# The feed-forward's input scale and rounding, moved from the attention steps into the preparation

## The chip, the core and the metric

The kernel runs on one core of one Trainium2 chip. The metric is device time in microseconds (us) from the start to the end of one execution; before the change it is 664.96 us, the median of 3 runs (664.12 to 666.36).

## What is computed

One transformer layer on x of shape (2, 1024, 256). The layer-normalised x goes to two branches that do not depend on each other, and the output is x plus both.

```python
xn = layernorm(x)                     # over the last axis, 2048 tokens of 256
# attention: 16 query heads, 4 key/value heads, causal, low-rank projections, rotary part of 64
# feed-forward with dynamic int8 rounding:
def dyn_quant_linear(x, w, b):
    sx = max(max(abs(x)) / 127, 1e-8)             # ONE scale for the whole tensor
    qx = clip(round(x / sx), -127, 127)
    sw = max(max(abs(w), axis=1) / 127, 1e-8)     # one scale per output channel
    qw = clip(round(w / sw[:, None]), -127, 127)
    return (qx @ qw.T) * (sx * sw) + b
h   = gelu(dyn_quant_linear(xn, w1, b1))          # w1: 1024 x 256
out = x + attention(xn) + dyn_quant_linear(h, w2, b2)
```

The scale sx needs the largest absolute value of the whole of xn, so nothing of xn can be rounded before all of it is normalised.

## The kernel before, in words

Five engines run their own programs and meet at semaphores. The order of each program is written out by hand; nothing is scheduled by a planner. There are three parts.

*Preparation* (from 0 to 69.7 us). The array `acc` (128 partitions, 16 tiles of 256) holds x, in four parts of 4 tiles. VectorE normalises it in place (`statistics`, `layernorm`, line 785), TensorE transposes it (`turn_xn`, line 1144), ScalarE and VectorE split the transposed values into a high and a low half (`xt_hi`, `xt_lo`), TensorE multiplies them down (`down`), and again both halves are stored (`down_low`, lines 809 to 813). Beside it the weights of the four key groups are folded: `turn_weights(g)`, `join_weights(g)` into PSUM bank 6, ScalarE's `weight_high(g)` (lines 611 to 617) and VectorE's `weight_low(g)` (lines 822, 825). GpSimd rotates and splits the first query (`rotate`, `split_query`, lines 490 to 508).

*Attention*, 32 steps (one head of one batch each) and a tail step. A step has six slots (`UNITS`), with two or one query tiles each. In a slot TensorE does `scores` (lines 1116 through `mm`), then values of the step before; VectorE does `maxima` (line 918) and, one slot later, `low` (line 926); ScalarE does `exponentials` (lines 700, 706); SyncE transposes the result by DMA (lines 374, 380). Scores of a unit wait for the `low` of the unit three before it. GpSimd turns the query of the step after next: four products of 2.3 to 2.4 us, a cast and a subtraction (line 508, which sets `qlo_done`; a step's first scores wait for it).

Work that belongs to no unit goes through "misc" entries: TensorE fills PSUM bank 6 or 7, alternately, and another engine empties it. `misc_of(n)` lists the entries of step n with their slots, in order, from a usual part and the table `EXTRA`; an entry waits (`misc_free`) until the entry two before it, which had the same bank, is emptied. Kinds: `query` (emptied by ScalarE, line 635), `turn` (the attention output of a pair of heads; emptied by ScalarE into o_hi and by VectorE into o_lo, line 950), `out`, `ka`, `kb`, and for the feed-forward `w` (transposed rounded weights, line 1382), `xmax` (the maxima of all partitions turned into a row by TensorE, `spread_rows`, line 1239) and `x` (transposed rounded xn, line 1375, emptied by ScalarE into `qx_t`, line 646).

The feed-forward's input is made ready inside the attention steps on VectorE: `largest(t)` (line 836) reduces a part of acc to its largest absolute value per partition, in slots 1 to 4 of step 2 (`LARGEST_AT`); line 1054 reduces the four; entry `xmax` in slot 5 spreads them; `activation_scale` (lines 987 to 991) makes sx, s1 = w1s * sx and 1/sx; `round_part(t)` (line 1010) rounds a part of acc in place, in slots 0, 2, 4 and 5 of step 3 (`ROUND_AT`). After the last `x` entry, in step 4, SyncE reloads x into acc (line 399), and the first additions of attention output to it come in step 5, slot 3 (line 956).

The scales of w1 and w2 are made in step 1 (`weight_largest`, lines 972 to 974), and GpSimd rounds both (lines 525, 529).

*Feed-forward and tail* (after 603 us): products, Gelu, scale, second rounding, output.

Of the kernel before, what the change touches and what calls it, by code (L numbers as in the profile page):

```python
# [117 lines left out]
def build(nc, x, w_kv_down, w_k_nope, w_k_rope, w_v, w_q_down, w_q_nope, w_q_rope, w_o, w1, b1, w2, b2,  # L118
          cos_rows, sin_rows, out):
    with ExitStack() as ctx:  # L120
# [638 lines left out]
        def _(dve):  # L759
# [223 lines left out]

            def activation_scale(idx):

                dve.wait_ge(S["misc_full"], idx + 1)
                dve.tensor_reduce(sm["xall"], misc_bank(idx)[:, 0:P], AX.X, ALU.max).then_inc(misc_used(idx), 1)
                dve.wait_ge(misc_used(idx), USERS_AHEAD[idx] + 1)
                chained(dve.tensor_scalar(sm["sx"], sm["xall"], 1.0 / QMAX, Q_EPS, ALU.mult, ALU.max))
                dve.tensor_scalar(sm["s1"], sm["w1s"], sm["sx"], None, ALU.mult)  # L990
                chained(dve.reciprocal(sm["rsx"], sm["sx"]))
# [13 lines left out]

            def round_part(t):

                part = acc[:, PT * t:PT * (t + 1), :].rearrange("p t d -> p (t d)")
                dve.wait_ge(S["xt_psum"], 2 * NPART)
                dve.tensor_scalar(part, part, sm["rsx"], MAGIC, ALU.mult, ALU.add).then_inc(S["x_rounded"], 1)  # L1010
# [503 lines left out]
```

## Time and profile before

| | us |
|---|---|
| median of 3 runs | 664.96 (664.12 to 666.36) |
| the profiled execution | 664.83 |
| its span, first to last instruction | 662.7 |
| busy: TensorE / VectorE / ScalarE / GpSimd | 581.1 / 524.5 / 460.4 / 459.7 |

The profile is of one execution. Its span is the time from the first to the last instruction; 2.1 us of the execution lie around it. In it PE is TensorE (PEld its weight loads), DVE VectorE, ACT ScalarE, POOL GpSimd, SP SyncE; PEclk is the clock granted to TensorE, 1.00 for 2.4 GHz and 0.50 for 1.2 GHz. A step is counted here from the start of its first `maxima` on VectorE: step 2 is 110.27 to 132.66 us, step 3 to 152.00, step 4 to 170.44.

### The profile page before, as it was taken

How to read it: one execution, taken by the hardware profiler on the slowest of the kernel's cores; microseconds unless marked ns; L12 is line 12 of the kernel's file. 1: busy time of each engine (PE TensorE's matmuls, PEld its weight loads, DVE VectorE, ACT ScalarE, POOL GpSimd, SP SyncE). 2: the span in 40 equal slices, each digit the busy share in tenths (PEclk: the TensorE clock that was granted, in tenths of full speed). 3: DMA queues.
4: the chain of work that ended last, by engine and by line, in shares of the span. 5: the costliest groups of instructions: out<-in, count | busy, mean ns of one | idle time of the engine just before them, and what ended most of it. 6: DMA issues, size and time to landing. Idle time of an engine off the chain costs nothing.

```text
span 662.7 us, 15774 instructions
## 1 busy us (share of the span) xinstructions
PE 581.1 (88%) x6288; PEld 423.3 (64%) x6288; DVE 524.5 (79%) x824; ACT 460.4 (69%) x712; POOL 459.7 (69%) x258
## 2 busy tenths in 40 slices
PE   7888888687979979997998899889899988986967
PEld 5566455465757657765776677667667765765536
DVE  5933778996768978897888788887988888885885
ACT  3445657668856867786778877876877688765762
POOL 3267777957766688768878977877797789730326
PEclk9868987989999989997999999999999999996979
DMA  9772796778999798899999999999999989998003
GB/s 258 231 238 82 184 195 119 122 141 168 211 161 170 156 166 155 147 156 182 167 163 154 170 154 171 159 180 168 163 157 165 160 154 157 156 155 141 17 1 127
DMA packets 323607, 104.13 MB, mean 157 GB/s; under 512 B 305808, under 2 KB 316624, under 8 KB 323408
## 3 DMA queue, kind: packets, MB, share of 16 engines
q1 hardware_dynamic: 322752, 102.54, 82.9%
q8 instruction: 50, 0.82, 0.5%
q10 hardware_dynamic: 784, 0.59, 0.3%
q14 instruction: 21, 0.17, 0.1%
HBM read 19.21 MB, written 8.39 MB: 42 GB/s over the span
## 4 chain that ended last, share of the span: by engine, by line
PE 39%; DVE 30%; ACT 10%; issue 8%; DMA 7%; POOL 4%; SPq 1%; DVEq 0%; POOLq 0%; ACTq 0%
PE psum L1116 36%; DVE small L918 10%; DVE p_src L926 8%; DMA pt<-p_src 5%; ACT psum L706 5%; ACT p_src L700 3%; DMA acc<-in_L_attn_x 3%; DVE o_lo L950 2%; PE psum L1329 1%; DVE small L1063 1%; SPq L380 1%; DVE o_norm L943 1%; DVE acc L785 1%; DVE acc L956 1%; POOL q_raw L496 1%
## 5 line engine op out<-in xcount | busy, mean ns | idle before, releaser
L700 ACT ACTIVATE p_src<-psum,small 128x1024 f16<-128x1024 f32 (+7 forms) x256 | 183.6, 743 | 134.9 <-DVE small L918 134.2
L918 DVE TENSOR_REDUCE small<-psum 128x1 f32<-128x1024 f32 (+7 forms) x256 | 186.8, 751 | 46.8 <-PE psum L1116 46.6
L926 DVE TENSOR_TENSOR p_src<-psum,p_src 128x1024 f16<-128x1024 f32 (+2 forms) x192 | 182.7, 951 | 30.1 <-ACT psum L706 29.0
L706 ACT ACTIVATE psum<-psum,small 128x1024 f32<-128x1024 f32 (+7 forms) x256 | 178.5, 720 | 0.0
L1116 PE MATMUL psum<-kv_tok,pt 128*128 128x65 f16 (+1 forms) x3456 | 142.4, 196 | 21.5 <-DMA pt<-p_src 11.1
L1116 PEld LDWEIGHTS psum<-kv_tok,pt 128*128 128x128 f16 x3456 | 127.1, 99 | 45.5 <-issue 16.6
L1116 PE MATMUL psum<-k_hi,q_hi 128*128 128x512 f16 (+3 forms) x384 | 126.5, 333 | 21.0 <-DVE p_src L926 12.2
L490 POOL TENSOR_TENSOR q_swap<-q_raw,sin_sb 32x1024 f32<-32x1024 f32 x32 | 75.3, 2353 | 81.7 <-ACT q_raw L635 81.3
L1116 PE MATMUL psum<-k_lo,q_hi 128*128 128x512 f16 (+3 forms) x384 | 127.3, 331 | 0.0
L1116 PE MATMUL psum<-k_hi,q_lo 128*128 128x512 f16 (+3 forms) x384 | 127.2, 331 | 0.0
L499 POOL TENSOR_TENSOR q_raw<-q_raw,q_swap 64x1024 f32<-64x1024 f32 x32 | 76.3, 2384 | 2.5
L493 POOL TENSOR_TENSOR q_swap<-q_raw,sin_sb 32x1024 f32<-32x1024 f32 x32 | 75.7, 2364 | 2.5
L496 POOL TENSOR_TENSOR q_raw<-q_raw,cos_sb 64x1024 f32<-64x1024 f32 x32 | 75.6, 2363 | 2.5
L1116 PEld LDWEIGHTS psum<-k_hi,q_hi 128*128 128x128 f16 x384 | 37.6, 98 | 54.0 <-issue 23.2
L508 POOL TENSOR_TENSOR q_lo<-q_raw,q_hi 128x1024 f16<-128x1024 f32 x32 | 68.4, 2136 | 2.6
L1116 PE MATMUL psum<-qc_hi,wq 128*128 128x512 f32 x120 | 53.8, 449 | 8.0 <-DVE o_lo L950 5.6
L1116 PE MATMUL psum<-cmask,ident 128*128 128x128 bf16 x256 | 56.7, 221 | 0.0
L1116 PEld LDWEIGHTS psum<-k_hi,q_lo 128*128 128x128 f16 x384 | 38.1, 99 | 27.4 <-issue 2.1
L635 ACT ACTIVATE q_raw<-psum,small 128x512 f32<-128x512 f32 x64 | 45.3, 707 | 5.8 <-PE psum L1116 5.7
L1116 PEld LDWEIGHTS psum<-k_lo,q_hi 128*128 128x128 f16 x384 | 38.1, 99 | 10.9 <-issue 0.8
L551 POOL TENSOR_TENSOR acc<-acc,b_row 128x512 f32<-128x512 f32 x8 | 9.9, 1272 | 43.0 <-DMA b_row<-in_L_ffn_b 31.9
L1116 PE MATMUL psum<-wvo_hi,o_hi 128*128 128x256 f32 x128 | 38.9, 304 | 0.9 <-DVE acc L956 0.9
(171 smaller groups left out, 894.5 us busy)
## 6 DMA issues: line engine op xcount, KB each, us to landing
pt<-p_src SPq DMA_TRANSPOSE x288, 3.6
wq_split<-w_split SPq DMA_DIRECT2D x4, 1024.0 KB, 5.1
wq<-wq_split SPq DMA_DIRECT2D x16, 256.0 KB, 3.6
acc<-in_L_attn_x SPq DMA_DIRECT2D x4, 512.0 KB, 7.5
ffn_t<-in_L_attn_W_o SPq DMA_DIRECT2D x1, 2048.0 KB, 19.3
k_rotated<-k_split SPq DMA_DIRECT2D x8, 256.0 KB, 2.6
w_sb<-in_L_ffn_w SPq DMA_DIRECT2D x2, 1024.0 KB, 7.1
acc<-in_L_attn_x SPq DMA_DIRECT2D x1, 2048.0 KB, 10.4
```

The source lines that it names most:

```text
L490: pool.tensor_tensor(q_swap[0:HR, :], raw[HR:ROPE, :], sin_sb[HR:ROPE, :], ALU.mult)\
L493: pool.tensor_tensor(q_swap[HR:ROPE, :], raw[0:HR, :], sin_sb[0:HR, :], ALU.mult)\
L496: pool.tensor_tensor(raw[0:ROPE, :], raw[0:ROPE, :], cos_sb[0:ROPE, :], ALU.mult)\
L499: pool.tensor_tensor(raw[0:ROPE, :], raw[0:ROPE, :], q_swap[:, :], ALU.add).then_inc(S["pool_step"], 1)
L508: pool.tensor_tensor(q_lo[n % 2][:, :], q_raw[n % 2][:, :], q_hi[n % 2][:, :], ALU.subtract)\
L635: act.activation(q_raw[s % 2][:, k * CH:(k + 1) * CH], misc_bank(idx), ACT.Copy, scale=sm["q_pow"])\
L700: ins = act.activation(p_src[u][:, 0, at:at + w], psum[:, COLS[i]:COLS[i] + w], ACT.Exp, bias=nb)
L706: ins = act.activation(ps, ps, ACT.Exp, bias=nb)
L918: dve.tensor_reduce(sm["mcol"][:, NT * (n % 2) + i:NT * (n % 2) + i + 1], psum[:, COLS[i]:COLS[i] + (i + 1) * P], AX.X, ALU.max, negate=True)\
L926: dve.tensor_tensor(p_src[u][:, 1, :], psum[:, o:o + WIDE[u]], p_src[u][:, 0, :], ALU.subtract)\
L950: dve.tensor_tensor(o_lo[pair][:, c], misc_bank(idx), o_hi[pair][:, c], ALU.subtract).then_inc(misc_used(idx), 1)
L1116: ins = pe.matmul(dst, lhs, rhs, start=start, stop=stop, skip_group_check=True)
```

## The change

The four `largest` and the reduction to one value per partition are issued in the preparation around `weight_low(1)`; the spread goes through bank 6 between `turn_xn(3)` and `turn_weights(2)` on TensorE; the scale and its inverse follow `xt_low(3)` on VectorE, and the four `round_part` stand at two places around `down_low` and `weight_low(2)`. The product s1 = w1s * sx moves to `weight_largest(0)` in step 1. The `xmax` entry is gone, and `x` entries stand in other slots: 0 and 2 in step 3, the other six in step 4, one in each slot.

```diff
-         2: [(0, "ka", 3), (2, "kb", 3), (3, "w", 0), (5, "w", 1), (5, "xmax", 0)],
-         3: [(3, "w", 2), (5, "w", 3), (5, "x", 0)],
-         4: [(0, "x", 1), (0, "x", 2), (2, "x", 3), (3, "x", 4), (3, "x", 5), (5, "x", 6), (5, "x", 7)],
+         2: [(0, "ka", 3), (2, "kb", 3), (3, "w", 0), (5, "w", 1)],
+         3: [(1, "x", 0), (3, "w", 2), (4, "x", 2), (5, "w", 3)],
+         4: [(0, "x", 1), (1, "x", 4), (2, "x", 3), (3, "x", 5), (4, "x", 6), (5, "x", 7)],
...
-LARGEST_AT = {(2, 1): 0, (2, 2): 1, (2, 3): 2, (2, 4): 3}
-ROUND_AT = {(3, 0): 0, (3, 2): 1, (3, 4): 2, (3, 5): 3}
...
             keys_products(1)
+            for t in range(NPART - 1):
+                largest(t)
             weight_low(1)
+            largest(NPART - 1)
+            dve.wait_ge(S["xpart_done"], NPART)
+            dve.tensor_reduce(sm["xrow"], sm["xmax"], AX.X, ALU.max).then_inc(S["xmax_done"], 1)
             xt_low(2)
             xt_low(3)
+            dve.wait_ge(S["xmax_spread"], 1)
+            dve.tensor_reduce(sm["xall"], bank[6][:, 0:P], AX.X, ALU.max).then_inc(S["xmax_read"], 1)
+            dve.wait_ge(S["xmax_read"], 1)
+            chained(dve.tensor_scalar(sm["sx"], sm["xall"], 1.0 / QMAX, Q_EPS, ALU.mult, ALU.max))
+            chained(dve.reciprocal(sm["rsx"], sm["sx"]))
...
+            dve.wait_ge(S["xt_psum"], 2 * NPART)
+            round_part(0)
+            round_part(1)
...
             down_low(3)
+            round_part(2)
             weight_low(2)
+            round_part(3)
             weight_low(3)
...
+                if k == 0:
+                    dve.tensor_scalar(sm["s1"], sm["w1s"], sm["sx"], None, ALU.mult)
...
+                    if g == 2:
+                        pe.wait_ge(S["xmax_read"], 1)
...
             turn_xn(3)
+            pe.wait_ge(S["xmax_done"], 1)
+            spread_rows(bank[6], sm["xrow"]).then_inc(S["xmax_spread"], 1)
             turn_weights(2)
```

How the programs of the engines stand at three places follows; line numbers of the changed kernel are its own.

VectorE in the preparation, before (the two key products, `weight_low(1)`, `xt_low`, `down_low`, `weight_low(2)`):

```order
L845 TENSOR_TENSOR kt_a<-psum,cos_sb 128x512
L848 TENSOR_TENSOR kt_b<-psum,sin_sb 128x512
L822 TENSOR_TENSOR w_split<-psum,w_split 128x4x64
L825 TENSOR_TENSOR w_split<-psum,w_split 64x4x64 x2
L802 TENSOR_TENSOR xt_lo<-psum,xt_hi 128x512 x4
L809 TENSOR_TENSOR qc_lo<-psum,qc_hi 128x512
L811 TENSOR_TENSOR qc_rest<-psum,qc_rest 64x512
L813 SCALAR_TENSOR_TENSOR k_lo<-psum,small,k_hi 64x512
L809 TENSOR_TENSOR qc_lo<-psum,qc_hi 128x512
L811 TENSOR_TENSOR qc_rest<-psum,qc_rest 64x512
L813 SCALAR_TENSOR_TENSOR k_lo<-psum,small,k_hi 64x512
L822 TENSOR_TENSOR w_split<-psum,w_split 128x4x64
```

and now:

```order
L846 TENSOR_TENSOR kt_b<-psum,sin_sb 128x512
L834 TENSOR_REDUCE small<-acc 128x1 x3
L820 TENSOR_TENSOR w_split<-psum,w_split 128x4x64
L823 TENSOR_TENSOR w_split<-psum,w_split 64x4x64 x2
L834 TENSOR_REDUCE small<-acc 128x1
L913 TENSOR_REDUCE small<-small 128x1
L800 TENSOR_TENSOR xt_lo<-psum,xt_hi 128x512 x4
L917 TENSOR_REDUCE small<-psum 128x1
L919 TENSOR_SCALAR small<-small 128x1
L920 RECIPROCAL small<-small 128x1
L925 TENSOR_SCALAR acc<-acc,small 128x1024 x2
L807 TENSOR_TENSOR qc_lo<-psum,qc_hi 128x512
```

Between the key product and `xt_low` stand five reductions, and between `xt_low` and `down_low` the scale and two roundings; the other two roundings stand ahead of `weight_low(2)` and of `weight_low(3)`.

VectorE in step 2 from the maxima of slot 4 to the first maxima of step 3, before:

```order
L926 TENSOR_TENSOR p_src<-psum,p_src 128x1024
L836 TENSOR_REDUCE small<-acc 128x1
L1054 TENSOR_REDUCE small<-small 128x1
L939 RECIPROCAL small<-psum 128x7
L943 TENSOR_TENSOR o_norm<-psum,small 128x7x64
L918 TENSOR_REDUCE small<-psum 128x1 x2
L926 TENSOR_TENSOR p_src<-psum,p_src 128x384
L987 TENSOR_REDUCE small<-psum 128x1
L989 TENSOR_SCALAR small<-small 128x1
L990 TENSOR_SCALAR small<-small 128x8
L991 RECIPROCAL small<-small 128x1
L918 TENSOR_REDUCE small<-psum 128x1
```

and now:

```order
L935 TENSOR_REDUCE small<-psum 128x1
L943 TENSOR_TENSOR p_src<-psum,p_src 128x1024
L956 RECIPROCAL small<-psum 128x7
L960 TENSOR_TENSOR o_norm<-psum,small 128x7x64
L935 TENSOR_REDUCE small<-psum 128x1 x2
L943 TENSOR_TENSOR p_src<-psum,p_src 128x384
L935 TENSOR_REDUCE small<-psum 128x1
```

Six rows are gone from this piece: line 836, line 1054 and lines 987 to 991.

TensorE in step 3, end of slot 1, before (the query product, then the scores of slot 2):

```order
L1116 MATMUL psum<-qc_hi,wq 128x512
L1116 MATMUL psum<-qc_lo,wq 128x512
L1116 MATMUL psum<-qc_hi,wq 128x512
L1116 MATMUL psum<-qc_rest,wq 128x512 x2
L1116 MATMUL psum<-k_hi,q_hi 128x512
L1116 MATMUL psum<-k_lo,q_hi 128x512
L1116 MATMUL psum<-k_hi,q_lo 128x512
L1116 MATMUL psum<-k_hi,q_hi 128x384
```

and now:

```order
L1112 MATMUL psum<-qc_hi,wq 128x512
L1112 MATMUL psum<-qc_lo,wq 128x512
L1112 MATMUL psum<-qc_hi,wq 128x512
L1112 MATMUL psum<-qc_rest,wq 128x512 x2
L1375 MATMUL psum<-identf,acc 128x128 x4
L1112 MATMUL psum<-k_hi,q_hi 128x512
L1112 MATMUL psum<-k_lo,q_hi 128x512
L1112 MATMUL psum<-k_hi,q_lo 128x512
L1112 MATMUL psum<-k_hi,q_hi 128x384
```

The transposes of entry x 0 now stand ahead of the scores of slot 2. The bank that they fill is the one of the first `turn` of the step, which VectorE empties in its slot 1 (line 950).

## Rows read from the trace of the kernel before

**Rows 1.** The page: busy time of the engines.

```profile
PE 581.1 (88%) x6288; PEld 423.3 (64%) x6288; DVE 524.5 (79%) x824; ACT 460.4 (69%) x712; POOL 459.7 (69%) x258
```

**Rows 2.** Stretches: steps 2, 3, 4 and 19; start:end, us, busy of each engine.

```profile
core 0: us, PE busy (x) PEld busy (x) DVE busy (x) ACT busy (x) POOL busy (x), PEclk, DMA share, GB/s
110.27:132.66 22.39, 17.05 (x187) 11.00 (x187) 21.61 (x31) 16.29 (x26) 20.84 (x12) 0.92 0.72 116
132.66:152.00 19.34, 15.47 (x161) 11.30 (x162) 17.20 (x25) 13.76 (x22) 12.26 (x6) 0.91 0.83 153
152.00:170.44 18.44, 15.83 (x196) 12.07 (x193) 12.17 (x18) 14.65 (x24) 11.58 (x7) 1.00 0.84 150
405.22:419.70 14.48, 12.81 (x157) 9.21 (x155) 13.02 (x21) 12.04 (x21) 12.01 (x7) 1.00 0.98 170
```

**Rows 3.** Timeline of VectorE, preparation: start, us, ..., idle before, releaser.

```profile
39.75 0.42 DVE L822 TENSOR_TENSOR w_split<-psum,w_split 128x256 fp32r<-128x256 f32 x1 [4.09 <-ACT w_split L617]
...
45.87 2.49 DVE L802 TENSOR_TENSOR xt_lo<-psum,xt_hi 128x512 fp32r<-128x512 f32 x4 [4.92 <-ACT xt_hi L578]
...
61.57 0.42 DVE L822 TENSOR_TENSOR w_split<-psum,w_split 128x256 fp32r<-128x256 f32 x1 [4.10 <-ACT w_split L617]
```

**Rows 4.** Line 836, the largest values; duration least/median/most in ns.

```profile
L836 DVE TENSOR_REDUCE small<-acc x4: 1206/1207/1209, 115.7 to 126.4; 128x1 f32<-128x1024 f32 x4
```

**Rows 5.** Timeline of VectorE, steps 2 and 3.

```profile
129.87 0.28 DVE L987 TENSOR_REDUCE small<-psum 128x1 f32<-128x128 f32 x1
...
130.38 2.19 DVE L990 TENSOR_SCALAR small<-small 128x8 f32<-128x8 f32 x1
...
132.66 1.23 DVE L918 TENSOR_REDUCE small<-psum 128x1 f32<-128x1024 f32 x1
...
137.99 1.08 DVE L918 TENSOR_REDUCE small<-psum 128x1 f32<-128x896 f32 x1
...
139.59 2.24 DVE L1010 TENSOR_SCALAR acc<-acc,small 128x1024 f32<-128x1024 f32 x1
```

**Rows 6.** Line 1010, the rounding.

```profile
L1010 DVE TENSOR_SCALAR acc<-acc,small x4: 744/764/2236, 135.0 to 150.2; 128x1024 f32<-128x1024 f32 x4
```

**Rows 7.** Timeline of GpSimd: preparation, step 1, step 2.

```profile
47.68 2.38 POOL L493 TENSOR_TENSOR q_swap<-q_raw,sin_sb 32x1024 f32<-32x1024 f32 x1
...
97.28 2.12 POOL L508 TENSOR_TENSOR q_lo<-q_raw,q_hi 128x1024 f16<-128x1024 f32 x1
...
123.85 2.12 POOL L508 TENSOR_TENSOR q_lo<-q_raw,q_hi 128x1024 f16<-128x1024 f32 x1
```

**Rows 8.** Timeline of TensorE, end of step 2, steps 3 and 4.

```profile
127.94 0.29 PE L1239 MATMUL psum<-identf,small 128*128 128x128 f32 x1 [1.14 <-DVE small L1054]
128.07 0.38 PE L1116 MATMUL psum<-k_hi,q_hi 128*128 128x512 f16 x1
...
144.67 0.80 PE L1116 MATMUL psum<-qc_hi,wq 128*128 128x512 f32 x1 [2.61 <-DVE o_lo L950]
...
150.45 0.38 PE L1116 MATMUL psum<-k_hi,q_hi 128*128 128x512 f16 x1 [0.79 <-issue]
...
165.55 0.50 PE L1116 MATMUL psum<-qc_hi,wq 128*128 128x512 f32 x1 [1.67 <-ACT ffn_t L646]
```

**Rows 9.** Timeline of VectorE, step 19, both o_lo of a turn.

```profile
409.74 0.68 DVE L950 TENSOR_TENSOR o_lo<-psum,o_hi 128x512 fp32r<-128x512 f32 x1
...
414.85 0.68 DVE L950 TENSOR_TENSOR o_lo<-psum,o_hi 128x512 fp32r<-128x512 f32 x1
```

**Rows 10.** Queue of SyncE, step 3: k_hi of batch 1 is fetched.

```profile
146.99 0.54 SPq L336 DMA_DIRECT2D k_hi<-k_rotated  x1
```

**Rows 11.** Timeline of VectorE, step 1, line 973.

```profile
96.31 0.92 DVE L973 TENSOR_SCALAR small<-small 128x8 f32<-128x8 f32 x1
...
107.58 0.17 DVE L973 TENSOR_SCALAR small<-small 128x2 f32<-128x2 f32 x1
```

**Rows 12.** Timeline of TensorE in the preparation: join_weights(3).

```profile
62.92 4.14 PE L1116 MATMUL psum<-wkv_t,wqn_t 128*128 128x64 f32 x16 [0.63 <-ACT wqn_t L601]
```

More of the change, by code:

```diff
@@ L259, in build @@
             wqr_hi wqr_lo kr_psum kr_ab kr_sum kr_hi kr_lo wd_squared norm_psum norm_read norm_pow k_scaled bound_in bound_psum rope_scaled kvt_psum kvt_hi kvt_lo wvo_psum wvo_hi_done
-            wvo_lo_done xpart_done xmax_done f_hrow_spread x_rounded w_scaled w_rounded w1q_done w2q_done
+            wvo_lo_done xpart_done xmax_done xmax_spread xmax_read f_hrow_spread x_rounded w_scaled w_rounded w1q_done w2q_done
             score_done max_done hi_done exp_done lo_done pv_done rest_done head_read misc_full misc6_used misc7_used
@@ L909, in _, with round_part @@
             keys_products(1)
+            for t in range(NPART - 1):
+                largest(t)
             weight_low(1)
+            largest(NPART - 1)
+            dve.wait_ge(S["xpart_done"], NPART)
+            dve.tensor_reduce(sm["xrow"], sm["xmax"], AX.X, ALU.max).then_inc(S["xmax_done"], 1)
             xt_low(2)
             xt_low(3)
+            dve.wait_ge(S["xmax_spread"], 1)
[3 more added lines that the diff above has]
+            chained(dve.reciprocal(sm["rsx"], sm["sx"]))
+            def round_part(t):
+                part = acc[:, PT * t:PT * (t + 1), :].rearrange("p t d -> p (t d)")
+                dve.tensor_scalar(part, part, sm["rsx"], MAGIC, ALU.mult, ALU.add).then_inc(S["x_rounded"], 1)
+            dve.wait_ge(S["xt_psum"], 2 * NPART)
+            round_part(0)
+            round_part(1)
             def maxima(n, u):
@@ L982, in wvo_low @@
                                          op0=ALU.mult, op1=ALU.subtract).then_inc(S["wvo_lo_done"], 1)
[L984 to L991, printed above, removed]
             def rotated_half(kind, n, idx):
@@ L1004, in rotated_half @@
                     dve.tensor_tensor(kt_a[0][:, :], kt_a[0][:, :], kt_b[:, :], ALU.add).then_inc(S["kr_sum"], 1)
[L1006 to L1010, printed above, removed]
             for n in range(LAST + 1):
@@ L1043, in _ @@
                             rotated_half(kind, k, misc_index(n, kind, k))
-                        if kind == "xmax":
-                            activation_scale(misc_index(n, kind, k))
                         if kind == "out":
                             add_out(1 - s // REP, k, misc_index(n, kind, k))
-                    if (n, j) in LARGEST_AT:
-                        largest(LARGEST_AT[n, j])
-                    if (n, j) in ROUND_AT:
-                        round_part(ROUND_AT[n, j])
-                    if (n, j) == max(LARGEST_AT):
-                        dve.wait_ge(S["xpart_done"], NPART)
-                        dve.tensor_reduce(sm["xrow"], sm["xmax"], AX.X, ALU.max).then_inc(S["xmax_done"], 1)
             normalise(LAST - 1, True)
@@ L1428, in _ @@
                             loop_keys(kind, k, idx)
-                        elif kind == "xmax":
-                            misc_free(idx)
-                            pe.wait_ge(S["xmax_done"], 1)
-                            spread_rows(misc_bank(idx), sm["xrow"]).then_inc(S["misc_full"], 1)
                         elif kind == "turn":
```

## The prediction

> **What bounds the kernel now.** I read the page first, then the stretches step by step, then the timelines of the engines in the steps that change. On the page TensorE is busy for 88% of the span, VectorE for 79% [rows 1]. That average hides the place that matters. In step 2 VectorE is busy 21.61 us of 22.39, in step 3 17.20 of 19.34, in step 4 only 12.17 of 18.44; step 19, which has the same usual work as step 3 and nothing extra, takes 14.48 [rows 2]. So steps 2 and 3 are bound by VectorE, and step 4 by no busy engine but by waits. GpSimd is close behind in step 2: 20.84 us busy. That is the engine that can take over there. In the preparation VectorE has holes: 4.09 us before `weight_low(1)`, 4.92 before `xt_low(2)`, 4.10 before `weight_low(2)` [rows 3]. A microsecond taken from VectorE in step 2 is worth a microsecond until GpSimd or TensorE is the later one; a microsecond put into a hole costs nothing while the hole lasts.
>
> **What goes from steps 2 and 3.** Step 2 loses four reductions of 1.21 us [rows 4], 4.8, and the scale, from the start of line 987 at 129.87 to the next maxima at 132.66, 2.8 [rows 5]. Together 7.6, or about 7.4 since neighbouring rows overlap by almost 0.1. Step 3 loses four roundings, 0.74 + 2 x 0.76 + 2.24 = 4.5 [rows 6]. In sum 11.9 us of VectorE. It does not all arrive.
>
> *Step 2.* Without 7.4 us VectorE would reach the maxima of step 3 at 132.66 - 7.4 = 125.3. But the scores of step 3 need the query's low half, which GpSimd finishes at 123.85 + 2.12 = 125.97 [rows 7], and nothing of GpSimd's work goes away in that step. Its work of step 2 began when the w2 scale of step 1 was ready, so it keeps its place. TensorE now begins those scores at 128.07, directly behind the spread row, which waited for line 1054 [rows 8]. It would begin at 126.0. The six products and the mask of that unit take 1.5 us together, an estimate from products of 0.38 that overlap by almost half [rows 8]. So the maxima start at 127.5 instead of 132.66: a gain of 5.2, with 2.2 us lost to GpSimd.
>
> *Step 3.* Entry x 0 now stands in slot 1, ahead of the scores of slot 2. Its bank was filled by the first `turn`, so it waits for VectorE's first o_lo. That is a new wait, and behind it in TensorE's queue stand the scores of slot 2, for which VectorE waits. In step 19 that o_lo ends at 409.74 + 0.68 = 410.42 [rows 9], 5.2 after the step's start at 405.22 [rows 2]. So here at 127.5 + 5.2 = 132.7; four transposes 0.5, the scores 1.3, and the third maxima start at 134.5. Now they start at 137.99 [rows 5]: the gain has shrunk to 3.5. Then the second o_lo, in step 19 at 415.53, 5.1 behind the first [rows 9]; from 132.7 with 1.5 of the new wait on top that is 139.3 to 139.7. It releases the second query product, which stands at 144.67 after a wait of 2.61 on that same o_lo [rows 8]: gain 5.0 again, since the long rounding of 2.24 was between [rows 5]. The first scores of step 4 start at 150.45 with 0.79 that no engine explains [rows 8]. They need k of batch 1, whose fetch SyncE issues at 146.99 [rows 10], 3.5 before; the fetch stands behind the transposes of unit 2 in SyncE's queue, which come behind VectorE's third low, and so moves with it. I take 5.0 at the start of step 4.
>
> *Step 4.* x entries now stand one to a slot. Before the second query product TensorE waits 1.67 us for ScalarE to empty a bank that was filled by the second of two x in slot 3 [rows 8]. In the new order the bank before that query is from slot 2, emptied long since. x 6 behind it may wait 0.3 for x 5. Of 1.67 I take 1.0, as ScalarE and VectorE follow at 14.65 and 12.17 us busy of 18.44 [rows 2]. Bounds 0 and 1.67. One x more in step 3, one fewer here: 0.5 us of TensorE either way, inside the numbers above. The reload of acc by SyncE stands behind the last transposes of step 4 both before and after and moves with them, so the additions of step 5 keep their distance.
>
> Gain in the steps: 5.0 + 1.0 = 6.0. Bounds: 2.1, what TensorE itself can start earlier (128.07 against 125.97), and 11.9 + 1.67 = 13.6, all of it.
>
> **What comes into the preparation.** The first three reductions, 3.6 us at 1.21 each [rows 4], fall into the hole of 4.09 before `weight_low(1)` at 39.75 [rows 3]. The fourth and the small one, 1.4, fall into the 4.92 before 45.87. The spread on TensorE is one transpose of 0.29 [rows 8] on the path to the first scores: 0.3, bounds 0.15 and 0.5. It waits for a maximum that is there about 42.4, four us before TensorE comes. `join_weights(2)`'s new wait on bank 6 is over by 50.
>
> The scale and two roundings then run beside GpSimd's rotation, whose products take 2.38 us each with 0.1 between [rows 7]. The trace shows such meetings. Line 973, eight numbers, takes 0.92 us and ends at 97.23, and GpSimd's next starts at 97.28; with GpSimd idle it takes 0.17 [rows 7, 11]. Line 990 takes 2.19 [rows 5], one rounding 2.24 against 0.76. A VectorE instruction of this kind waits until GpSimd's instruction ends. With that, the first rounding, issued near 49.4, runs when the product of 47.68 ends at 50.06, the second behind it or behind the next product, at the latest done near 53.7. `down_low` then follows 3 us later than now, but it has pauses of 2.5 of its own, and 4.10 stand before `weight_low(2)` at 61.57 [rows 3]. `join_weights(3)` starts at 62.92 [rows 12], and needs `weight_low(2)`; ScalarE's copy releases it now, by a hair. So I cost the roundings at 0. If the cover is gone: five instructions at 2.24 + 0.1 wait, 11.7 us, against a cover of 4.10 + 4.9, so at most 2.7.
>
> **What comes into step 1.** s1 is line 990 with its 2.19 us [rows 5], now behind line 973. In step 1 VectorE's chain is as tight as in step 2, and its w2 scale starts GpSimd's second rounding, which leads to the 125.97 above: what s1 costs moves everything. It would be issued near 97.26, GpSimd's line 508 starts at 97.28 and holds for 2.12 [rows 7]. If VectorE is first it costs 0.2; if second 2.2. Neither is nearer by the rows, with 0.02 us between; I take 1.2.
>
> *A rule weighed.* The rows give this wait only as durations. The Trainium skill, SBUF — State Buffer, section "SBUF: two separate sides", says that VectorE and GpSimd share a pair of ports under an exclusive lock, held for a whole instruction, and that whoever starts first has it. By that rule s1 costs either bound, never the middle, and GpSimd is held too, which would delay the rotation beside the two roundings. The durations of lines 973, 990 and 1010 agree with it. By the rule at its worst the sum below would be 1.0 us later.
>
> **The sum.** 6.0 gained, 0.3 + 1.2 = 1.5 paid, net 4.5. The profiled execution took 664.83 us, its span 662.7, so it stands 0.13 below the median of the runs. 664.83 - 4.5 = 660.3; on the median's scale 660.5.
>
> **The rivals.**
> *A, GpSimd decides more than I think.* Steps 3 and 4 keep only the 2.1 us of TensorE, plus 1.0 in step 4, less 1.5: 664.83 - 1.6 = 663.2. For it: GpSimd's 20.84 of 22.39 [rows 2]. Against it: in step 3 GpSimd is busy only 12.26 us, so its lead returns.
> *B, all arrives.* GpSimd is no bound and the new bank wait is nothing: 13.6 - 1.5 = 12.1, 652.7. For it: VectorE's saturation. Against it: 125.97 stands in the trace.
> *C, the shared lock takes it back.* Paid 0.5 for the spread, 2.7 in the preparation and 2.2 for s1, 5.4 against 6.0: 664.2. For it: 2.19 and 2.24; against it: holes of 4.10 and 4.92 us. It decides from the point at which `weight_low(2)` ends after 62.9.
> *D, slower: the bank waits.* x 0 and x 2 in step 3 and x 6 in step 4 stand ahead of scores, and each waits for another engine to empty its bank. If each costs what the worst such wait costs now, 2.61 [rows 8], and goes round through scores, maxima and the next bank, 7.8 is paid in place of the 1.5 counted in my walk, against the 5.2 of step 2 and the 1.5 paid before: 664.83 + 7.8 - 5.2 + 1.5 = 668.9. It decides from 1.2 us a wait. For it: the order of TensorE's program is fixed, so a wait holds scores too. Against it: in step 19 the o_lo is early, and x 2's bank is emptied by ScalarE, which has slack.
>
> **How the numbers follow.** My forecast 0.60, A 0.14, B 0.08, C 0.10, D 0.08. What can be told from no change is 0.3%, 2.0 us, thus below 662.97 is faster. Forecast, B and nearly half of A are faster: 0.74. C and the rest of A are same: 0.18. D is slower: 0.08. The forecast's own range is 658.3 to 662.4 (s1 0.2 to 2.2, step 4 0 to 1.67, step 3 by 1 either way). The range for 8 in 10 reaches over A to C: 656.8 to 664.4, and leaves B and D out.
>
> **What would show it.** Right: maxima of step 3 start 16.5 to 18 us after those of step 2 (22.39 now), behind GpSimd's line 508; TensorE waits for o_lo ahead of x 0; steps 3 and 4 together take about 37 us (37.8 now); the first maxima at 69.7 + 0.3; s1 shows 0.2 or 2.2. Wrong: first maxima after 71 (C), waits above 1.2 before x 2 or x 6 (D), a step 2 of 15 us or less (B), or a gain at the start of step 4 that is gone by step 8, because a later wait was fixed in time.

## The result: 662.2 us, ratio 0.994

The changed kernel takes 662.17 us in the median of 20 runs (659.2 to 668.8); the kernel before takes 666.22 beside it, also 20 runs. The ratio is 0.994, 95% interval 0.991 to 0.997: faster by 0.6%, just beyond what can be told from no change. The ratios here and below are taken over the runs within 1.5% of each kernel's fastest, which leaves out one run of 803.68 us of the kernel before and five of the twelve of `x0_later`, whose medians of all runs give 0.995. The profiled execution took 660.75 us (before 664.83), 4.1 less; 4.5 was forecast. The terms are less good than their sum.

All kernels here are compared by the starts of their steps. A step starts with VectorE's first maxima of it (line 918 before, line 935 after); the times are us between two such starts.

| | first maxima at | step 0 | step 1 | step 2 | step 3 | step 4 | steps 0 to 4 | steps 5 to 30 |
|---|---|---|---|---|---|---|---|---|
| before | 69.68 | 19.49 | 21.10 | 22.39 | 19.33 | 18.45 | 100.76 | 419.99 |
| after | 70.86 | 19.97 | 22.53 | 17.28 | 19.97 | 16.38 | 96.12 | 419.13 |
| gain | -1.18 | -0.48 | -1.43 | 5.11 | -0.64 | 2.07 | 4.64 | 0.86 |

The page of the profile after, busy time of the engines, beside [rows 1]:

```profile
PE 578.4 (88%) x6288; PEld 421.7 (64%) x6288; DVE 526.5 (80%) x824; ACT 460.3 (70%) x712; POOL 459.3 (70%) x258
```

VectorE has the same 824 instructions and is busy 2.0 us longer, though the program ends earlier. Work was not saved, it was moved. Steps 1 to 4 of the changed kernel, as stretches, which answer to [rows 2]:

```profile
core 0: us, PE busy (x) PEld busy (x) DVE busy (x) ACT busy (x) POOL busy (x), PEclk, DMA share, GB/s
90.83:113.36 22.53, 17.23 (x207) 12.40 (x208) 19.58 (x26) 10.88 (x19) 16.94 (x16) 0.85 0.69 125
113.36:130.64 17.28, 14.33 (x156) 9.30 (x156) 15.55 (x22) 13.89 (x23) 16.38 (x10) 1.00 0.78 120
130.64:150.60 19.96, 15.71 (x200) 11.83 (x197) 13.39 (x20) 16.48 (x27) 15.05 (x8) 1.00 0.93 176
150.60:166.99 16.39, 15.06 (x192) 11.61 (x189) 12.11 (x19) 14.14 (x23) 11.87 (x6) 1.00 0.87 154
```

In step 2 VectorE's busy time fell from 21.61 to 15.55, and the step became 5.1 shorter. In step 3 it fell from 17.20 to 13.39, and the step became *longer*: 6.6 us of 19.96 VectorE now waits. (TensorE's granted clock is 0.91 in step 3 before [rows 2] and 1.00 after, so the clock doesn't explain the longer step.) That is the place to look. TensorE's waits in it, those of [rows 8] after:

```profile
136.92 0.66 PE L1375 MATMUL psum<-identf,acc 128*128 128x128 f32 x4 [2.15 <-DVE o_lo L967]
...
144.36 0.51 PE L1112 MATMUL psum<-qc_hi,wq 128*128 128x512 f32 x1 [1.17 <-DVE o_lo L967]
...
146.13 0.66 PE L1375 MATMUL psum<-identf,acc 128*128 128x128 f32 x4 [0.34 <-ACT ffn_t L648]
...
149.06 0.38 PE L1112 MATMUL psum<-k_hi,q_hi 128*128 128x512 f16 x1 [0.59 <-issue]
```

The first is entry x 0, ahead of the scores of slot 2: the new wait, and 2.15 us of it. The third is x 2. VectorE in the same place, beside [rows 5]:

```profile
136.18 0.68 DVE L967 TENSOR_TENSOR o_lo<-psum,o_hi 128x512 fp32r<-128x512 f32 x1
138.80 1.09 DVE L935 TENSOR_REDUCE small<-psum 128x1 f32<-128x896 f32 x1 [1.94 <-PE psum L1112]
```

It makes the o_lo for which TensorE stands, and then stands 1.94 us itself for the scores that TensorE issues behind x 0. The last wait of TensorE, 0.59 that no engine explains, is the fetch of k, as experiment 3 shows.

The end of step 2, TensorE and GpSimd:

```profile
128.12 0.62 PE L1382 MATMUL psum<-ident,ffn_t 128*128 128x128 bf16 x8 [1.01 <-ACT ffn_t L646]
129.08 0.39 PE L1112 MATMUL psum<-k_hi,q_hi 128*128 128x512 f16 x1 [0.33 <-POOL q_lo L506]
```

```profile
126.89 2.12 POOL L506 TENSOR_TENSOR q_lo<-q_raw,q_hi 128x1024 f16<-128x1024 f32 x1
```

q_lo ends at 129.01, the scores of step 3 start at 129.08, the maxima at 130.64. The last releaser is GpSimd, as forecast, but TensorE had already stood 1.01 us for ScalarE right before it.

In step 1, VectorE and GpSimd, s1 at line 994, beside [rows 7, 11]:

```profile
97.97 0.28 DVE L992 TENSOR_SCALAR small<-small 128x8 f32<-128x8 f32 x1
98.28 2.17 DVE L994 TENSOR_SCALAR small<-small 128x8 f32<-128x8 f32 x1
100.36 0.19 DVE L995 RECIPROCAL small<-small 128x8 f32<-128x8 f32 x1
```

```profile
98.30 2.12 POOL L506 TENSOR_TENSOR q_lo<-q_raw,q_hi 128x1024 f16<-128x1024 f32 x1
100.78 0.48 POOL L523 TENSOR_SCALAR w_sb<-w_sb,small 128x256 f32<-128x256 f32 x1 [0.37 <-DVEq L996]
```

s1 takes as long as GpSimd's instruction beside it, and GpSimd's next one then waits 0.37 for the reciprocal.

### The profile page after: what moved, and what is told of

Its sections match the earlier page's. It is cut to its first block, busy times and chain, and to the rows that moved or that the text cites. A ratio compares the mean times of both kernels' runs of the same rounds, so it can differ in the third digit from the quotient of the medians.

```text
span 658.4 us, 15774 instructions
## 1 busy us (share of the span) xinstructions
PE 578.4 (88%) x6288; PEld 421.7 (64%) x6288; DVE 526.5 (80%) x824; ACT 460.3 (70%) x712; POOL 459.3 (70%) x258
## 4 chain that ended last, share of the span: by engine, by line
PE 41%; DVE 27%; ACT 10%; issue 8%; DMA 7%; POOL 4%; SPq 1%; DVEq 0%; POOLq 0%; ACTq 0%
PE psum L1112 38%; DVE small L935 9%; DVE p_src L943 8%; ACT psum L704 5%; DMA pt<-p_src 5%; ACT p_src L698 3%; DMA acc<-in_L_attn_x 3%; DVE o_lo L967 2%; PE psum L1329 1%; DVE small L1059 1%; SPq L378 1%; DVE acc L783 1%; DVE o_norm L960 1%; POOL q_raw L494 1%; POOL q_swap L488 1%
## 5 line engine op out<-in xcount | busy, mean ns | idle before, releaser
L1112 PE MATMUL psum<-kv_tok,pt 128*128 128x65 f16 (+1 forms) x3456 | 140.7, 195 | 22.1 <-DMA pt<-p_src 13.4
L1112 PEld LDWEIGHTS psum<-kv_tok,pt 128*128 128x128 f16 x3456 | 125.4, 99 | 45.4 <-issue 17.7
L633 ACT ACTIVATE q_raw<-psum,small 128x512 f32<-128x512 f32 x64 | 45.4, 709 | 5.3 <-PE psum L1112 5.2
```

Source lines behind the costliest of these rows:

```text
L633: act.activation(q_raw[s % 2][:, k * CH:(k + 1) * CH], misc_bank(idx), ACT.Copy, scale=sm["q_pow"])\
L1112: ins = pe.matmul(dst, lhs, rhs, start=start, stop=stop, skip_group_check=True)
```

## The experiments

Their times are medians, each beside the kernel before on the same chip (666.5 us in the first group, 667.2 in the second, 667.7 in the third). The steps, in us:

| | first maxima | step 0 | 1 | 2 | 3 | 4 | steps 0 to 4 |
|---|---|---|---|---|---|---|---|
| s1_at_w2 | 73.88 | 19.90 | 20.67 | 18.42 | 20.02 | 16.38 | 95.40 |
| x0_later | 73.92 | 19.85 | 22.64 | 17.28 | 19.31 | 16.38 | 95.46 |
| both | 69.64 | 19.48 | 21.34 | 17.30 | 19.73 | 16.39 | 94.23 |
| old_slots | 73.72 | 19.75 | 22.74 | 17.30 | 20.26 | 18.66 | 98.71 |
| keys_fetched_earlier | 69.97 | 19.17 | 21.09 | 17.31 | 17.31 | 17.22 | 92.11 |
| no_prep_work | 69.70 | 19.48 | 23.30 | 18.46 | 19.47 | 16.38 | 97.09 |
| w2_not_scaled | 70.02 | 19.80 | 22.70 | 17.29 | 20.21 | 16.38 | 96.38 |
| new_slots_only | 70.09 | 19.11 | 20.97 | 24.82 | 20.76 | 16.43 | 102.09 |
| fetch_only | 70.99 | 19.98 | 22.53 | 17.28 | 19.22 | 17.13 | 96.14 |
| query_earlier | 70.07 | 19.49 | 23.24 | 17.40 | 17.51 | 17.22 | 94.85 |
| three_edits_again | 69.66 | 19.47 | 21.35 | 17.30 | 17.31 | 17.22 | 92.66 |

In all of them the steps 5 to 30, whose program is the same, take 417.2 to 421.0 together. That spread is as wide as the effects looked for, so a small loss there would not be seen: keys_fetched_earlier takes 1.2 us more in them than the changed kernel, query_earlier 1.9 less.

**1. The two things that came in: s1_at_w2, x0_later, both.**

```diff
 # s1_at_w2: s1 behind the scale of w2
-                if k == 0:
+                if k == 1:
                     dve.tensor_scalar(sm["s1"], sm["w1s"], sm["sx"], None, ALU.mult)
 # x0_later: x 0 in slot 4, x 2 in slot 5
-         3: [(1, "x", 0), (3, "w", 2), (4, "x", 2), (5, "w", 3)],
+         3: [(3, "w", 2), (4, "x", 0), (5, "w", 3), (5, "x", 2)],
```

> The changed kernel, with s1 = w1s * sx made in the scale of w2 (step 1, slot 4), ahead of its reciprocal, where GpSimd sits idle until that scale is ready, and not in the scale of w1, where it showed 2.17 us beside GpSimd's query work. Theory (the 2.17 us are a wait for GpSimd's instruction, on the path): the instruction shows about 0.17 us, step 1 takes 20.5 us where the changed kernel's trace has 22.5, and the time is 2.0 us below the changed kernel's, a ratio to the kernel before of about 0.991. Rival (the 2.17 cover waits for ScalarE that come out again, 1.33 us stand behind it): step 1 stays at 22 or more, and the ratio stays at 0.994.

> The changed kernel, with x 0 in slot 4 of step 3 behind the second query product and x 2 in slot 5 behind w 3; the rest as it is. Theory (x 0 in slot 1 waits 2.15 us for o_lo and holds up the scores of slot 2, for which VectorE waits 1.94): the first wait is gone, the maxima of slot 2 start 6 us after the step's start and not 8.2, and steps 3 and 4 together take 34.4 us in place of 36.35; ratio about 0.991. Rival (the wait moves: x 0 then waits for w 2's bank and x 2 for x 0's, ahead of step 4's scores): steps 3 and 4 stay at 36 together and the ratio at 0.994.

> Both edits at once: s1 in the scale of w2, x 0 in slot 4 and x 2 in slot 5 of step 3. If both waits are on the path and independent, 3.9 us below the changed kernel, ratio about 0.988. If GpSimd bounds step 2 and what follows, the second adds nothing to the first: 0.991.

Measured: s1_at_w2 663.0 us (ratio 0.993, 0.990 to 0.997), x0_later 663.5 (0.990, 0.985 to 0.994), both 660.6 (0.989, 0.986 to 0.993). With s1 away from GpSimd's instruction step 1 takes 20.67 and 21.34, with it 22.53 and 22.64. What blurs the comparison is the scale of w1 just before it (line 992; 973 before, 982 in no_prep_work). In every trace it ends 0.02 to 0.03 us after an instruction of GpSimd, and so takes from 0.28 to 1.03:

```profile
96.27 1.01 DVE L992 TENSOR_SCALAR small<-small 128x8 f32<-128x8 f32 x1
```

```profile
96.32 1.03 DVE L982 TENSOR_SCALAR small<-small 128x8 f32<-128x8 f32 x1
```

The first is of `both`, the second of no_prep_work; the changed kernel's 0.28 stands above. Without this row step 1 takes 22.25 to 22.27 in all six kernels with s1 beside GpSimd's q_lo, 20.32 or 20.33 in the four with s1 behind the w2 scale and GpSimd idle, and 20.18 or 20.19 in the two with the computing of before. So s1 costs 1.9 us there and 0.15 behind the w2 scale, where it takes 0.23 and step 2 of `both` still takes 17.30. TensorE's clock isn't seen in it: s1_at_w2 has none of step 1 at the lower level, `both` 3.8 us, and the two agree. (All six with the 22.25 have 6.8 us of it, so how much those would cost alone isn't shown.) The 18.42 of s1_at_w2 isn't s1's, as experiment 4 shows.

x0_later takes the o_lo wait away, and step 3 still takes 19.31. TensorE and SyncE's queue in `both`, step 3:

```profile
145.94 0.38 PE L1112 MATMUL psum<-k_hi,q_hi 128*128 128x512 f16 x1 [2.25 <-issue]
```

```profile
141.89 0.54 SPq L334 DMA_DIRECT2D k_hi<-k_rotated  x1
142.48 0.59 SPq L335 DMA_DIRECT2D k_lo<-k_rotated  x1
143.16 4.07 SPq L372 DMA_TRANSPOSE pt<-p_src  x2
```

The wait without a name has grown from 0.59 to 2.25, and ends 3.46 us after the issue of k_lo. Steps 3 and 4 together take 35.7 in x0_later, not the 34.4 expected: the gain went into the fetch.

**2. What gives what: old_slots, new_slots_only.** The changed computing with the two rows of the table from before, and the computing of before with the two new rows.

```diff
 # old_slots (after, with these rows); new_slots_only is the reverse, on before
-         3: [(1, "x", 0), (3, "w", 2), (4, "x", 2), (5, "w", 3)],
-         4: [(0, "x", 1), (1, "x", 4), (2, "x", 3), (3, "x", 5), (4, "x", 6), (5, "x", 7)],
+         3: [(3, "w", 2), (5, "w", 3), (5, "x", 0)],
+         4: [(0, "x", 1), (0, "x", 2), (2, "x", 3), (3, "x", 4), (3, "x", 5), (5, "x", 6), (5, "x", 7)],
```

> The changed kernel with the x entries in the slots of the kernel before (x 0 in slot 5 of step 3, seven in step 4); maxima, scale and rounding stay in the preparation. Theory (the computing moved gives the gain of step 2, the slots only shift 2 us from step 4 to step 3): step 2 stays 17.3, step 3 about 18, step 4 about 18.4, ratio 0.994 as the changed kernel. Rival (the slots carry the gain): ratio 0.997 or more.

> The kernel before with the new slots of the x entries; maxima, scale and rounding stay in steps 2 and 3. Theory (moved computing gives step 2, new slots give step 4): step 2 stays 22.4, step 3 19.3 to 20, step 4 16.4 in place of 18.45; ratio about 0.997. Rival (slots pay only when VectorE is free): step 4 stays at 18.4, ratio 1.000.

Measured: old_slots 666.0 (ratio 0.997, 0.993 to 1.000), new_slots_only 668.9 (1.003, 1.000 to 1.006). With the old slots step 2 is at 17.30 and step 4 at 18.66; with the new slots alone step 4 is at 16.43. TensorE in step 4 of old_slots:

```profile
167.54 0.51 PE L1112 MATMUL psum<-qc_hi,wq 128*128 128x512 f32 x1 [1.67 <-ACT ffn_t L644]
```

That is the 1.67 of [rows 8], to the hundredth. So the computing moved gives step 2, and the slots give step 4. The cleanest pair for their size is the kernel before and new_slots_only, 18.45 and 16.43 with a granted clock of 1.00 in both; in the 18.66 of old_slots it is 0.94. Step 3 of old_slots was expected at 18 and takes 20.26: TensorE stands 2.85 ahead of step 4's scores, with no engine as releaser, the kind of wait that experiment 3 takes away.

By themselves the new slots show no gain in the times, where 0.997 was expected: what step 4 wins, step 3 mostly pays, 20.76 against 19.33. It has the same wait for o_lo,

```profile
140.45 0.89 PE L1375 MATMUL psum<-identf,acc 128*128 128x128 f32 x4 [2.35 <-DVE o_lo L950]
```

with VectorE's roundings still in it. Their step 2, 24.82, isn't a clean reading: the edit doesn't touch it, and TensorE's granted clock is 0.73 in it, against 0.92 in [rows 2]. Steps 1, 3 and 4 together are 0.7 us shorter than before, so it isn't shown that the slots alone make the kernel slower.

**3. The fetch of k: keys_fetched_earlier, fetch_only.** SyncE issues store and fetch of batch 1's k one unit earlier in step 3, on `both` and on the changed kernel.

```diff
-                        if u == 1 and n in STORED_IN:
+                        if u == (0 if n == 3 else 1) and n in STORED_IN:
                             store_keys(STORED_IN[n])
-                        if u == 2 and n == 3:
+                        if u == 1 and n == 3:
                             first_keys(1)
```

> Both edits (s1 in the scale of w2; x 0 and x 2 later in step 3), and in SyncE's queue of step 3 the store of the rotated keys behind unit 0 and the fetch of k of batch 1 behind unit 1, one unit earlier each. In the trace of both edits TensorE stands 2.25 us before the first scores of step 4 with no engine as releaser, and they start 3.5 us after the fetch's second issue. Theory (step 3 now ends on that fetch, which is why taking away the wait for o_lo gave 0.2 to 0.7 us and not 2): step 3 takes 17.5 us, the wait is under 0.3, and the time is 2.2 below both edits; ratio about 0.986. Rival (the wait is for something else, or the transposes pushed back cost as much): step 3 stays at 19.3 to 19.7 and the ratio at 0.989.

> The changed kernel with only the store and fetch of the rotated keys one unit earlier in SyncE's queue of step 3; s1 and the x entries as it has them. Theory (the wait for o_lo ahead of x 0 and the fetch are two limits of step 3, one close behind the other): the wait of 0.59 us before step 4's first scores goes, step 3 takes 19.4 in place of 19.97, where with x 0 later as well it took 17.3; ratio 0.993. Rival (the fetch alone bounds step 3): 17.5 here too, ratio 0.991.

Measured: keys_fetched_earlier 659.9 (ratio 0.991, 0.987 to 0.995), fetch_only 662.3 (0.990, 0.985 to 0.995). The intervals don't tell the kernels of this section from each other or from the changed one; the steps do. Steps 2 to 4 of keys_fetched_earlier:

```profile
110.23:127.54 17.31, 15.74 (x158) 9.72 (x156) 14.76 (x22) 13.92 (x23) 16.42 (x10) 0.91 0.71 121
127.54:144.86 17.32, 15.52 (x200) 11.83 (x197) 13.30 (x21) 15.57 (x26) 14.79 (x8) 1.00 0.93 172
144.86:162.07 17.21, 15.22 (x192) 11.71 (x189) 12.19 (x18) 14.90 (x25) 12.16 (x6) 1.00 1.00 171
```

Step 3 falls to 17.3, 2.4 below `both`, and no wait without a name is left; step 4 takes 0.8 more. Its SyncE queue and TensorE's three waits that are left in steps 3 and 4:

```profile
139.51 0.54 SPq L334 DMA_DIRECT2D k_hi<-k_rotated  x1
140.10 0.59 SPq L335 DMA_DIRECT2D k_lo<-k_rotated  x1
```

```profile
138.91 0.50 PE L1112 MATMUL psum<-qc_hi,wq 128*128 128x512 f32 x1 [1.18 <-DVE o_lo L967]
...
146.58 0.66 PE L1375 MATMUL psum<-identf,acc 128*128 128x128 f32 x4 [0.66 <-ACT ffn_t L648]
158.40 0.66 PE L1375 MATMUL psum<-identf,acc 128*128 128x128 f32 x4 [1.33 <-ACT ffn_t L644]
```

Steps 3 and 4 together: changed kernel 36.35, the fetch earlier alone 36.35, x 0 later alone 35.7 (36.1 in `both`), the two together 34.5. Two limits stand one behind the other; either taken away alone gives 0 to 0.7 us, the two 1.8. In fetch_only the step 3 wait for o_lo is still 2.15, and the 0.75 that step 3 gains step 4 pays back.

**4. The preparation: no_prep_work.** All that came into the preparation is left out (maxima, spread row, scale, the four roundings; the input isn't rounded). s1 stays in step 1, with another factor.

```diff
-            for t in range(NPART - 1):
-                largest(t)
...
-                dve.tensor_scalar(part, part, sm["rsx"], MAGIC, ALU.mult, ALU.add).then_inc(S["x_rounded"], 1)
+                dve.sem_inc(S["x_rounded"], 1)
```

> The changed kernel without anything that it added to the preparation: no maxima, no spread, no scale, no rounding (s1 takes another factor), so the feed-forward's input is not rounded; the steps are unchanged. Theory (the work fits into VectorE's holes; 1.0 us of the 1.2 by which the first maxima come later in the changed kernel's trace is TensorE's clock at 1.2 GHz for 20.5 us in place of 17.1): nothing is won but 0.1 to 0.3 us for the spread; first maxima at 69.6, or near 73.9 where the clock is also low early; ratio 0.994. Rival (the lock shared with GpSimd makes the moved roundings cost 1 us or more, rival C): ratio 0.991 or less.

Measured: 662.1 (ratio 0.993, 0.990 to 0.996). First maxima at 69.70 without the work, at 69.64 and 69.66 with all of it (`both`, three_edits_again). The work costs nothing there. Its step 2 came out at 18.46, though nothing in that step was changed, and s1_at_w2 had 18.42. Both have 3.4 us at TensorE's lower level late in the step; here as stretches of no_prep_work, the whole step 2 and that part of it:

```profile
112.48:130.94 18.46, 15.85 (x156) 9.92 (x156) 15.56 (x23) 15.08 (x25) 17.57 (x10) 0.91 0.81 120
127.20:130.60 3.40, 3.36 (x14) 1.66 (x15) 2.43 (x6) 2.87 (x7) 3.24 (x3) 0.50 1.03 105
```

In keys_fetched_earlier and three_edits_again such 3.4 us lie at the start of step 2, and it takes 17.31 and 17.30; the changed kernel has none there and takes 17.28. So the late stretch costs step 2 some 1.1 us, and the early one nothing. Step 1 takes 23.30, 0.77 more than in the changed kernel, with the same 6.8 us at the lower level in it: 0.75 of it is the w1 scale, 1.03 against 0.28 (experiment 1).

**5. What bounds step 2: w2_not_scaled, query_earlier.** The first leaves out GpSimd's w2 roundings (w2's integers are wrong by that). The second, on keys_fetched_earlier, moves the queries of step 1 a slot forward and w2's integers behind them, into step 2.

```diff
 # w2_not_scaled
+                if k == 1:
+                    pool.sem_inc(S["w_rounded"], 1)
...
 # query_earlier
-        usual += [(2, "query", 0), (5, "query", 1)] if n == 1 else [(1, "query", 0), (4, "query", 1)]
+        usual += [(1, "query", 0), (4, "query", 1)]
...
+                if n == 2:
                     weight_integers(1, w2_sb, w2q, D // P, "w2q_done")
```

> The changed kernel without GpSimd's scaling and rounding of w2 in step 1 (2.21 us; w2 goes on unscaled, which changes the feed-forward's values). Theory 1 (GpSimd alone ends step 2 and sets the gain, as the prediction's sum has it): scores of step 3 start 2.2 us earlier and step 2 takes 15.1 us. Theory 2 (from the changed kernel's trace: TensorE waited only 0.33 us for the query, behind 1.01 us for ScalarE's copy of w 0): GpSimd, ScalarE and TensorE stand within 0.4 us of each other, and step 2 takes 16.9 us or more.

> The kernel with all three edits (s1 in w2's scale, x 0 and x 2 later, keys fetched earlier), and in step 1 the two query products in slots 1 and 4 in place of 2 and 5, with GpSimd's rounding of w2 behind the rotation for step 3 in place of ahead of it. In every trace so far GpSimd's rotation for step 3 is released by ScalarE's copy of that second product, even where w2's scaling is left out (GpSimd then stood 2.55 us for it). Theory 1 (TensorE is 0.35 us behind GpSimd there, held by ScalarE's copy of w 0): q_lo of step 3 is ready 5 us or more before it is needed, and step 2 takes 16.9 in place of 17.3; ratio as with three edits. Theory 2 (the relay from ScalarE's copy through GpSimd alone holds step 2): step 2 takes 16 us or less.

Measured: w2_not_scaled 661.4 (ratio 0.995, 0.991 to 0.998), query_earlier 662.4 (0.989, 0.984 to 0.995). Step 2 takes 17.29, as theory 2 of w2_not_scaled has it, and 17.40, which neither theory of query_earlier has. GpSimd in w2_not_scaled:

```profile
114.89 2.38 POOL L488 TENSOR_TENSOR q_swap<-q_raw,sin_sb 32x1024 f32<-32x1024 f32 x1 [2.55 <-ACT q_raw L635]
```

Freed of the roundings it stands 2.55 us for ScalarE's copy of the query, and ends where it ended. In query_earlier GpSimd has q_lo ready at 118.53, 9.8 us before step 3's first scores at 128.31, and TensorE waits behind ScalarE instead:

```profile
116.39 2.14 POOL L506 TENSOR_TENSOR q_lo<-q_raw,q_hi 128x1024 f16<-128x1024 f32 x1
```

```profile
127.86 0.62 PE L1383 MATMUL psum<-ident,ffn_t 128*128 128x128 bf16 x8 [0.59 <-ACT ffn_t L647]
```

So GpSimd's q_lo is the last releaser of step 3 in the changed kernel, but taking it away didn't make step 2 shorter. One thing stands beside that reading: in query_earlier 4.6 us of step 2 are at TensorE's lower level, and TensorE is busy 16.81 of 17.40:

```profile
112.80:130.20 17.40, 16.81 (x183) 11.06 (x181) 13.89 (x23) 13.27 (x22) 11.42 (x9) 0.87 0.77 118
```

`both` and keys_fetched_earlier bear some 3 us of it at the start of the step without loss; whether 4.6 hide a gain here, no run tells. In the changed kernel's own trace GpSimd is worth at most the 0.33 that TensorE waits for it behind ScalarE's 1.01. What makes the step 17.3 long, then, is probably the ring of scores, maxima, exponentials and banks over TensorE, VectorE and ScalarE, which also feeds GpSimd. That is argued and not shown, and which bank or engine in it decides stays open. The edit also made step 1 longer, 23.24, where TensorE stood 4.63 us for VectorE's o_norm (2.14 in `both`). GpSimd's products now run where s1 stands, and s1 is held once more, beside one that starts at 108.06:

```profile
108.04 2.38 DVE L995 TENSOR_SCALAR small<-small 128x8 f32<-128x8 f32 x1
```

So its place behind the w2 scale is cheap only while GpSimd is idle there, and as a version query_earlier is worse.

**6. The best version once more: three_edits_again** is keys_fetched_earlier, with the same source.

> The kernel with all three edits once more, beside the others on one chip. Its step table had 92.1 us for steps 0 to 4 where the changed kernel had 96.1 and the kernel before 100.8, so 4.0 us below the changed kernel and a ratio to the kernel before of about 0.988; if the three edits only shift waits, 0.994.

Measured: 658.8 (ratio 0.988, 0.982 to 0.994); steps 0 to 4 take 92.66, against 96.12 in the changed kernel and 100.76 before. By these steps it is the best version, 3.5 to 4.0 us below the changed kernel; by the whole span of the two traces, 2.8 and 3.2 (655.6 and 655.2 against 658.4). In the timed runs its interval overlaps that kernel's 0.991 to 0.997, so they don't show that it is faster than the changed kernel.

## Why the prediction was right, and where its terms were not

- *Step 2, 5.2 forecast, 5.11 measured.* Right in size and in what is seen: maxima of step 3 17.28 us after those of step 2, behind line 506 (508 before). Wrong in the reason given, that GpSimd's work starts with the w2 scale and so keeps its place: w2_not_scaled took the roundings behind that scale away and step 2 didn't move, as GpSimd's rotation waits for ScalarE's copy of the query; query_earlier took GpSimd out and it didn't move, though at a lower clock. Rival B, a step 2 of 15 us or less, is refuted by the 17.28.
- *Step 3, -0.2 forecast, -0.64 measured.* The wait for o_lo was foreseen at 1.5 and is 2.15. The recovery behind it was put at 5.0 of the 5.2 because the long rounding stood between the two o_lo; the second o_lo still holds the query product for 1.17, and then comes the fetch. I had SyncE's issue "move with" the third low and treated it as harmless. It is a limit of its own: in the kernels with a wait for it, the scores start 2.9 to 3.5 us after the issue of k_lo.
- *Step 4, 1.0 forecast, 2.07 measured.* The mis-sized term. I took 1.0 of 1.67 as the other engines follow close; new_slots_only shows that the slots alone give it (18.45 against 16.43). It isn't simply the 1.67 that went. Two shorter waits for ScalarE went too, 0.69 and 0.25, neither of which was in the walk:

```profile
156.00 0.47 PE L1116 MATMUL psum<-qc_hi,wq 128*128 128x512 f32 x1 [0.69 <-ACT ffn_t L646]
...
162.21 0.66 PE L1375 MATMUL psum<-identf,acc 128*128 128x128 f32 x4 [0.25 <-ACT ffn_t L646]
```

  And x 6, put at 0.3, now waits 1.33 for ScalarE to empty the bank of x 5,

```profile
163.31 0.66 PE L1375 MATMUL psum<-identf,acc 128*128 128x128 f32 x4 [1.33 <-ACT ffn_t L644]
```

  So TensorE's idle time in the step fell by 1.3, from 2.6 to 1.33, and its busy time by 0.8, from the 15.83 of [rows 2] to 15.06, with one entry fewer. I had called that entry 0.5 "either way" and left it out of the sum. What either would have given alone, no run here tells.
- *s1, 1.2 forecast, 2.17 for the instruction.* I had bounds of 0.2 and 2.2 and took the middle, which neither end allows. The step became 1.43 longer, so the sum was off by 0.2 only, and that is luck: without the w1 scale it became 2.07 longer (20.18 to 22.25), and the scale, by where GpSimd's cast happened to end, took 0.28 instead of 0.92 [rows 11] and gave 0.64 back.
- *Preparation, 0.3 forecast, 1.18 measured.* The two roundings ran beside GpSimd as said, one of them in 2.89, and were done at 53.63, where 53.7 was the latest forecast. They cost nothing: rival C falls there. VectorE's last hole is still 3.17 of the 4.10 in [rows 3]:

```profile
49.89 3.74 DVE L925 TENSOR_SCALAR acc<-acc,small 128x1024 f32<-128x1024 f32 x2
...
62.92 0.42 DVE L820 TENSOR_TENSOR w_split<-psum,w_split 128x256 fp32r<-128x256 f32 x1 [3.17 <-ACT w_split L615]
```

  The 1.18 isn't the change's but for some 0.1 for the spread row, since `both` with all the work starts at 69.64. It goes with TensorE's clock (below) and an input that landed 0.2 later. So does the 0.48 of step 0: in the kernels whose step 0 starts after the lower level has ended it takes 19.47 to 19.49, the one before among them, and in those that start 0.3 to 0.8 us ahead of its end 19.75 to 19.98. (Two kernels that start 2.4 to 2.5 us ahead of its end have no second stretch in the step, and take 19.11 and 19.17.)
- *Rival D* named the right place and the right wait, 2.15 against its price of 2.61. It didn't decide, although its conditions came true: x 6 waits more than the 1.2 that was named as a sign against the forecast, and the three x entries wait 2.15, 0.34 and 1.33, together 3.8 where D was to decide from 3 times 1.2. What D had wrong is that it adds the waits to all that were there: the 2.61 before the second query product fell to 1.17, and the 1.67, 0.69 and 0.25 of step 4 went. In new_slots_only, where VectorE's work hadn't left, step 3 shows this rival alone, 1.4 longer than before.
- The net came out because errors cancel: +1.1 in step 4 and +0.9 in steps 5 to 30, against 0.9 in the preparation, 0.5 in step 0, 0.4 in step 3, 0.2 in step 1, 0.1 in step 2 and 0.2 outside the span. The 0.9 in steps 5 to 30 is within what these steps vary by from kernel to kernel, so it is luck too. What was claimed for steps 3 and 4 together, 37 us, is 36.35.

## What to carry to other kernels

When work leaves an engine that is busy 97% of a step, the step falls only to its next limit; look at what runs beside it in the same step, not at the average. A step that waits often has two limits in series (here a bank, then a fetch): one removed alone shows little or nothing, so try the two together before calling either harmless. And where an order is fixed, moving entries so that none stands behind a bank just filled can be worth as much as moving arithmetic: here 2.0 us of one step for two rows of a table, once VectorE's work had made room in the step before.
